# Three token groups' partial sums added by accumulating transfers instead of GpSimd adds, in the selective-scan stage of a graph and state-space block

## The reference, cut to what matters

```
dA = exp(dt[:, :, None] * A[None])                       # 4096 x 512 channels x 16 states
dBu = dt[:, :, None] * B[:, None, :] * u[:, :, None]
def step(hst, inp):
    dAt, dBut, Ct = inp
    hst = dAt * hst + dBut
    return (hst, hst @ Ct)                               # y[token, channel] = sum over 16 states of h * C
y = ys + u * D_skip
y = y * silu(z)
return y @ w_out
```

## Time and profile before

| | |
|---|---|
| median of 3 runs | 2358.94 us |
| the profiled execution, its own time | 2360.41 us |
| its span in the profile | 2358.5 us |
| TensorE busy (matmul) | 2189.1 us, 93% |
| VectorE busy | 1803.0 us, 76% |
| ScalarE busy | 1566.7 us, 66% |
| GpSimd busy | 1146.6 us, 49% |
| scan steps, first to last start | 1106.7 to 2126.4 us |
| mean share of the 16 DMA engines in use, 1186 to 1860 us | about 0.32 |

### The profile page before, as it was taken

How to read it: one execution, slowest core, us unless ns; L and a number is a source line. 1 busy time by engine, 2 the same in 40 slices (tenths; PEclk the granted TensorE clock), 3 DMA queues, 4 the chain that set the end, 5 groups by cost and what they waited for, 6 DMA issues and landing times.

```text
span 2358.5 us, 26231 instructions
## 1 busy us (share of the span) xinstructions
PE 2189.1 (93%) x8900; PEld 1393.1 (59%) x8900; DVE 1803.0 (76%) x2083; ACT 1566.7 (66%) x2541; POOL 1146.6 (49%) x928
## 2 busy tenths in 40 slices
PE   7999999999999999989999999998999987787998
PEld 4544545555555556456766666676766664444886
DVE  5666767777777765324999998999989998996665
ACT  5577686777686845425676767677676868775444
POOL 2101322222231313213988888888988888890000
PEclk9999999999999999999999999999999999898999
DMA  6243332323232323233323232323323221312121
GB/s 234 72 134 102 108 116 90 125 96 122 87 125 88 119 90 134 83 107 109 131 93 125 90 125 89 117 99 107 117 100 125 90 83 43 117 36 98 36 81 45
DMA packets 117495, 241.22 MB, mean 102 GB/s; under 512 B 8770, under 2 KB 66370, under 8 KB 116978
## 3 DMA queue, kind: packets, MB, share of 16 engines
q1 hardware_dynamic: 108290, 207.14, 26.4%
q0 software_dynamic: 8528, 31.36, 3.8%
q10 hardware_dynamic: 544, 1.05, 0.1%
HBM read 219.20 MB, written 20.32 MB: 102 GB/s over the span
## 4 chain that ended last, share of the span: by engine, by line
PE 65%; ACT 10%; POOL 10%; DVE 10%; issue 5%; DMA 0%; ACTq 0%; DVEq 0%; POOLq 0%
PE ps L685 13%; PE ps L727 10%; POOL dB L2306 6%; PE ps L971 5%; DVE h L1473 3%; PE ps L849 2%; PE ps L823 2%; PE ps L955 2%; POOL acc L2288 2%; PE ps L709 2%; ACT ps L1659 2%; ACT L1657 1%; POOL du L2302 1%; PE ps L755 1%; PE ps L753 1%
## 5 line engine op out<-in xcount | busy, mean ns | idle before, releaser
L1473 DVE TENSOR_TENSOR_SCAN h<-ps,hst,dB 128x512 f32<-128x512 f32 x512 | 636.9, 1270 | 59.0 <-ACT ps L1659 50.5
L2306 POOL TENSOR_TENSOR dB<-du,bc 128x512 f32<-128x512 f32 x512 | 648.0, 1287 | 61.6 <-DVE h L1473 59.1
L685 PE MATMUL ps<-wgt,msg 128*128 128x512 f32 x1024 | 489.0, 598 | 2.1 <-DVE xb L1181 2.1
L1659 ACT ACTIVATE ps<-dt,cols 128x512 f32<-128x512 f32 x512 | 351.9, 692 | 181.1 <-DVE h L1473 178.8
L727 PE MATMUL ps<-raw,msg 128*128 128x256 f32 x1792 | 436.3, 379 | 0.9 <-ACT hb L1659 0.9
L971 PE MATMUL ps<-consts,h 128*128 128x128 f32 x2048 | 318.9, 281 | 70.7 <-DVE acc L1435 38.0
L971 PEld LDWEIGHTS ps<-consts,h 128*128 128x128 f32 x2048 | 251.6, 144 | 224.8 <-DVE acc L1435 73.4
L727 PEld LDWEIGHTS ps<-raw,msg 128*128 128x128 f32 x1792 | 324.0, 190 | 74.1 <-issue 42.1
L685 PEld LDWEIGHTS ps<-wgt,msg 128*128 128x128 f32 x1024 | 190.0, 192 | 206.2 <-issue 204.6
L1659 ACT ACTIVATE wgt<-wgt 128x1024 f32<-128x1024 f32 x256 | 257.9, 1046 | 51.9 <-DVE wgt L1146 50.5
L2288 POOL TENSOR_TENSOR acc<-acc,part 128x512 f32<-128x512 f32 x174 | 226.4, 1301 | 59.7 <-ACT part L1659 58.3
(11 more groups left out here) (320 smaller groups left out, 3589.9 us busy)
## 6 DMA issues: line engine op xcount, KB each, us to landing
raw<-in_adjT SPq DMA_DIRECT2D x256, 512.0 KB, 3.4
bc<-tmp_bc SPq DMA_DIRECT2D x64, 512.0 KB, 4.6
E<-tmp_bc POOLq DMA_DIRECT2D x32, 512.0 KB, 4.1
xb<-in_xT POOLq DMA_DIRECT2D x8, 512.0 KB, 4.1
tmp_x<-xb POOLq DMA_DIRECT2D x8, 512.0 KB, 4.2
x<-tmp_x SPq DMA_DIRECT2D x8, 512.0 KB, 5.8
tmp_x<-x SPq DMA_DIRECT2D x8, 512.0 KB, 4.8
msg<-in_W SPq DMA_DIRECT2D x4, 1024.0 KB, 10.6
```

The lines of the kernel that those rows point to most:

```text
L685: x = e.matmul(P[d][:, :], msg[:, j, d * 128:(d + 1) * 128], wgt[g % NW][:, l, :], start=j == 0, stop=j == NJ - 1)
L1473: e.tensor_tensor_scan(hr[n % 3][:, m, :], PS[4 + k % 2].t[:, :], dBr[k % 4][:, :], hst[:, n % 16, m:m + 1], ALU.mult, ALU.add).then_inc(S ...
L1659: return e.activation(out, in_, func, bias=bias, scale=scale)
L2306: e.tensor_tensor(dBr[k % 4][:, :], du[:, m, :], bcr[i % 3][:, n % 2, :], ALU.mult).then_inc(S("dB"), 1)
```

## The change

Parts of groups 0, 1 and 2 are added to `acc` by DMA transfers with an add ("moved"), states 1 to 12 of groups 0 and 1 and states 1 to 11 of group 2. ScalarE writes the parts of all three groups. GpSimd issues the transfers in two chains ("lanes"): groups 0 and 1 in one transfer of two parts, group 2 in one of its own. A transfer is issued at `j + 11` of the last group in its lane; for the last moved state of a lane it is `j + 8`. Each chain has two buffers for parts and one semaphore. To make room, `x3` becomes a view of `xcb` and `th1` becomes `sq1`, with the waits that this needs. `post_b` gets one more slot. Over the whole run 257 units are moved, in 90 transfers of the first lane and 83 of the second; VectorE adds 184, TensorE 40, and ScalarE starts 31.

```diff
@@ adder
-    if s == 0:
-        return "gpsimd" if n < 14 else "vector"
-    if s == 1:
-        return "gpsimd" if 2 <= n < 13 else "vector"
+    if s < 3:
+        return "moved" if n < (13 if s < 2 else 12) else "vector"
     return "vector"
+LANES = ((0, 1), (2,))
+def moved_of(ib, n, lane):
+    return [s for s in LANES[lane] if adder(ib, n, s) == "moved"]
+MOVED = [{x: i for i, x in enumerate((ib, n) for ib in range(NB) for n in range(16) if moved_of(ib, n, lane))} for lane in range(2)]
+def landed(j):
+    ib, n, s = unit(j)
+    return 16 * (MOVED[s // 2][ib, n] + 1)
@@ tiles
-        part = [sb(cB, f"part{i}", [128, 512]) for i in range(2)]
+        part = [[sb(cB, f"part{lane}{i}", [128, len(LANES[lane]), 512]) for i in range(2)] for lane in range(2)]
-        x3 = sb(cB, "x3", [128, 2, TB])
-        th1 = sb(cB, "th1", [128, 2, TB])
+        x3 = xcb[:, 0:2, 3:TB + 3]
+        th1 = sq1
@@ order
-        NP, NPA, NSA, NPB, NPO = 64, 55, 62, 71, 18
+        NP, NPA, NSA, NPB, NPO = 64, 55, 62, 71, 19
-        post_load = [1] * 8 + [0, 0] + mean_var
+        post_load = [1] * 8 + [0, 0] + mean_var + [0]
@@ SyncE, post_b, ahead of the load of x3
+                w.wait_ge(S("halo1"), min(ib + 2, NB))
@@ ScalarE, pre_b, ahead of the write of xcb
                         w.wait_ge(S("halo1"), ib)
+                        w.wait_ge(S("d_xn3"), 16 * (ib - 1))
+                        w.wait_ge(S("sum"), 2 * (ib - 1))
@@ ScalarE, post_b, ahead of the normalization
+                w.wait_ge(S("th1r"), 2 * min(ib + 2, NB))
@@ VectorE, gather
-                        if last in HANDED:
-                            w.wait_ge(S("summed"), HANDED[last] + 1)
+                        if adder(*unit(last)) == "moved":
+                            w.wait_ge(S(f"d_acc{s // 2}"), landed(last))
@@ ScalarE, gather
-                    elif how == "gpsimd":
-                        w.wait_ge(S("summed"), HANDED[j] - 1)
-                        act(part[HANDED[j] % 2][:, :], b.ps[:, :], ACT.Copy, scale=c).then_inc(b.evac, 1)
+                    elif how == "moved":
+                        lane, i = s // 2, MOVED[s // 2][ib, n]
+                        w.wait_ge(S(f"d_acc{lane}"), 16 * (i - 1))
+                        act(part[lane][i % 2][:, s - LANES[lane][0], :], b.ps[:, :], ACT.Copy, scale=c).then_inc(b.evac, 1)
@@ GpSimd
-            def add(j):
-                ib, n, s = unit(j)
-                made, last = hT_use(j), hT_use(j - 4)
-                w.wait_ge(made.evac, made.n)
-                if j - 4 in HANDED:
-                    w.wait_ge(S("summed"), HANDED[j - 4] + 1)
-                else:
-                    w.wait_ge(last.evac, last.n)
-                e.tensor_tensor(acc[:, s, :], acc[:, s, :], part[HANDED[j] % 2][:, :], ALU.add).then_inc(S("summed"), 1)
+            def add(ib, n, lane):
+                ss = moved_of(ib, n, lane)
+                for s in ss:
+                    made, last = hT_use(64 * ib + 4 * n + s), hT_use(64 * ib + 4 * n + s - 4)
+                    w.wait_ge(made.evac, made.n)
+                    if n > 1:
+                        w.wait_ge(S(f"d_acc{lane}"), landed(64 * ib + 4 * n + s - 4))
+                    else:
+                        w.wait_ge(last.evac, last.n)
+                e.dma_start(acc[:, ss[0]:ss[-1] + 1, :], part[lane][MOVED[lane][ib, n] % 2][:, 0:len(ss), :],
+                            accum_op=ALU.add).then_inc(S(f"d_acc{lane}"), 16)
             for k in range(64 * NB + HAND):
-                if k - HAND in HANDED:
-                    add(k - HAND)
+                for behind in (HAND, HAND - 3):
+                    if k >= behind:
+                        ib, n, s = unit(k - behind)
+                        if s < 3 and moved_of(ib, n, s // 2)[-1:] == [s]:
+                            if (behind == HAND) == (n < 15 and (ib, n + 1) in MOVED[s // 2]):
+                                add(ib, n, s // 2)
```

More of the change, by code:

```diff
@@ L48, in unit @@
     return j // 64, j % 64 // 4, j % 4
-HANDED = {j: i for i, j in enumerate(j for j in range(64 * NB) if adder(*unit(j)) == "gpsimd")}
+LANES = ((0, 1), (2,))
[5 more added lines that the diff above has]
+    return 16 * (MOVED[s // 2][ib, n] + 1)
 SUMMED = {j: i for i, j in enumerate(j for j in range(64 * NB) if adder(*unit(j)) == "tensor")}
@@ L440, in build @@
                   (gate_use(NB - 1, 3).full, gate_use(NB - 1, 3).n), (postb_use(NB - 1, 3).evac, postb_use(NB - 1, 3).n),
-                  (S("rr3"), 2 * NB), (S("gate"), 4 * NB), (S("summed"), len(HANDED)), (S("d_x3s"), 16 * NB), (S("d_xn3"), 16 * NB), (S("d_bcs"), 16 * NB)]
+                  (S("rr3"), 2 * NB), (S("gate"), 4 * NB), *((S(f"d_acc{lane}"), 16 * len(MOVED[lane])) for lane in range(2)), (S("d_x3s"), 16 * NB), (S("d_xn3"), 16 * NB), (S("d_bcs"), 16 * NB)]
         @block.sync
@@ L813, in outer @@
                     yield
-                    w.wait_ge(S("setup"), 5)
+                    w.wait_ge(S("setup"), 7)
                     w.wait_ge(Y.evac, Y.n - 1)
@@ L988, in gates @@
                             last, how = hT_use(64 * ib + 60 + s), adder(ib, 15, s)
-                            if how == "gpsimd":
-                                w.wait_ge(S("summed"), HANDED[64 * ib + 60 + s] + 1)
-                            elif how == "tensor":
+                            if how == "tensor":
                                 w.wait_ge(sum_use(ib, s).evac, sum_use(ib, s).n)
@@ L1117, in _ @@
             w.wait_ge(S("d_consts"), 32)
-            e.tensor_copy(col("cw0", 16, 4)[64:128, :], col("cw0", 20, 4)[0:64, :]).then_inc(S("taps"), 1)
-            e.tensor_copy(col("cb0", 4)[64:128, :], col("cb0", 5)[0:64, :]).then_inc(S("taps"), 1)
+            e.tensor_copy(col("cw0", 16, 4)[64:128, :], col("cw0", 20, 4)[0:64, :]).then_inc(S("setup"), 1)
+            e.tensor_copy(col("cb0", 4)[64:128, :], col("cb0", 5)[0:64, :]).then_inc(S("setup"), 1)
             w.wait_ge(S("Aexp"), 1)
@@ L1210, in pre_a @@
                 e.scalar_tensor_tensor(dt, sm[:, 2, :], 0.0, sm[:, 3, :], ALU.max, ALU.add).then_inc(S("dt"), 1)
-                w.wait_ge(S("setup"), 1)
+                w.wait_ge(S("setup"), 3)
                 w.wait_ge(S("dt"), ib + 1)
@@ L1220, in pre_a @@
                     w.wait_ge(b.evac, b.n)
-                    w.wait_ge(S("taps"), 2)
+                    w.wait_ge(S("setup"), 2)
                     e.tensor_scalar(c, xbc[:, m, 0:TB], col("cw0", 4 * m), col("cb0", m), ALU.mult, ALU.add).then_inc(S("conv"), 1)
```

## The result

The changed kernel takes **2431.76 us** (median of 4 runs, 2429.82 to 2433.62) against 2359.43 for the kernel before beside it: a ratio of **1.0306** (95% interval 1.0288 to 1.0324). It is slower, as forecast, but by 72 us where 12 were forecast, and above the upper end of its range, 2396.

What follows compares the result with a forecast made beforehand. TensorE was taken to bound the long stretches, GpSimd and VectorE full at 1337 to 1374 us. Six blocks at +2.4 us (+14.4), block 6 -1.9, block 7 -4.3 and +4.2: +12.4, so 2371 us; range from a little under 2334 to 2396.

Steps and rivals of the forecast that it cites:

- last transfer of the first lane: Step 49, iteration 57: GpSimd has time by then, counted at 0, up to 2 us; landings counted hidden.
- Last transfer of group 2: Step 46, issued in iteration 54: `dB` of step 54 waits for ScalarE's part and the issue, +2.6 us a block.
- ScalarE's parts: 11 more per block at 0.7 us, hidden in TensorE's stretches; the one at step 49 costs +0.3 us.
- -0.7 for the short chain: One add fewer on VectorE shortens the ScalarE and VectorE chain before 1416.0 us, -0.7 us a block.
- `post_b`'s +0.5: Two sums move from the block's end to step 25, beside the short chain: 0 to 1.2 us, taken as +0.5.
- An issue: On GpSimd, taken as 0.57 us like a plain one, other end 1.31; GpSimd 18 us lighter a block.
- rival D: GpSimd is not relieved: an issue costs 1.3 us, as an add did; 2376 us, no chance given.
- VectorE's adds: Per block 36 become 25, 8 us less, mostly worth nothing under TensorE or ScalarE; -0.7 and +0.7 us counted.
- Blocks 6 and 7: Block 6, not TensorE-bound: -1.9 us. Block 7: six adds off full VectorE -4.3, two late last transfers +4.2.
- Shared tiles: New waits for `x3` in `xcb` and `th1` in `sq1` are for work already finished in program order: 0.
- A: Rival, faster: late `dB` of step 54 is covered by ScalarE's bound, the full stretch shrinks; 2334 us, chance 0.35.
- C: Rival: transfers land after more than 8.3 us behind two adjacency loads; 2413 us at 9 us, chance 0.07.

Runs made afterwards that it cites:

- e5: Against e1, group 2's adds go back to VectorE, leaving only the first lane's transfers, last ones at 11: 2371.55 us, ratio 1.0058.
- e1: Against the changed kernel, the last transfer of each lane is issued 11 steps behind its unit instead of 8: 2378.39 us, ratio 1.0087.
- e7: Against the changed kernel, only the first lane's last transfer goes to 11 steps behind, group 2's stays at 8: 2412.21 us, ratio 1.0224.
- e11: Against e5, the first lane's last transfer is issued 8 steps behind its unit, group 2 still on VectorE: 2380.27 us, ratio 1.0089.
- e4: Against the kernel before, only the shared tiles, their waits and the extra post slot, no accumulating transfer: 2360.67 us, ratio 1.0009.
- e8: Against the kernel before, group 2 moved by transfers at 11 in blocks 6 and 7 only, GpSimd's adds kept: 2359.32 us, ratio 1.0002.

## Why the prediction was wrong

**The step that failed** is the last transfer of the first lane, by way of its landing: "A chain's next transfer waits for the one before, four steps later (8.3 us at 133.1 / 64) ... I count it hidden", and "The first lane's last one (step 49, iteration 57) ... I count it at 0, up to 2 us". The distance of four steps holds for all transfers of a lane but the last, and the last is issued three iterations early, as the paragraph before it in the prediction says. 11 - 8 = 3 of the four steps are gone. One step is 2.1 us; by that sum even the 4.2 us of a plain transfer would have left 2.1 where 0 was counted. What came in its place is a landing of 8.66 us, most of it in the open, and an idle VectorE of 6.7 us, of which 2.8 a block remain in the time.

This is the largest of three terms that were too small. Taken one step at a time, the runs split the block like this (us a block):

| part of the change | in the prediction | measured |
|---|---|---|
| first lane at 11, shared tiles (e5 less before) | -0.7 - 0.3 + 0.7 + 0.5 = +0.2 | 133.5 - 133.1 = +0.4 |
| group 2's lane, at 11 (e1 less e5) | +0.3 - 0.7 = -0.4 | 135.8 - 133.5 = +2.3 |
| group 2's last transfer at 8 (e7 less e1) | +2.6 | 139.9 - 135.8 = +4.1 |
| first lane's last transfer at 8 (changed kernel less e7) | 0 | 142.7 - 139.9 = +2.8 |
| sum | +2.4 | +9.6 |

Point by point:

- **First lane's last transfer, 0.** Wrong: 2.8 a block on top of group 2's, 1.7 alone (e11). Two things were left out. One is the landing, 5.1 us of the wait at step 57. The other is the row of exponential, part, issue and `dB` that the prediction had found at step 54: at step 57 it makes the scan 3.3 us late by itself in e11, where the landing ends together with the part, and the softplus addition did not cover it.
- **Last transfer of group 2, +2.6.** The mechanism was right, at the step named, and the size too small: the scan is 3.3 us late, where 2.5 were counted (3.3 was the end with the dear issue), and the early issue costs 4.1 a block. The sum left out that the issue also slows the `dB` behind it (1.88 us in the row at 1351.35, 1.29 counted). Why 3.3 us late costs 4.1 is not shown.
- **ScalarE's parts, +0.3, "in TensorE's stretches they are hidden".** Too small. With the -0.7 for the short chain, group 2's lane was counted at -0.4 a block and measured at +2.3; the scans' wait for the exponential grows with it (37.1 to 52.6 us in 850). `post_b`'s +0.5 is in line with e4's block of 133.6, though that execution was 3.7 us slower than e4's median.
- **An issue, 0.57, with 1.31 as the other end.** The next instruction starts 0.61 us after the issue (1347.69 to 1348.30), but the next `dB` takes 0.3 to 0.6 longer: 0.9 to 1.2 us of GpSimd in all, nearer rival D's end. `dB`'s mean rose from 1291 ns to 1503. GpSimd's busy time in a block fell to 528.8 / 5 = 105.8, not to 98: it is 10 us lighter, not 18.
- **VectorE's adds.** 184 are left, as said, and its idle time grew by more than what they took. That this relief is worth little in blocks 0 to 5 is in line with the runs (group 2's lane, which brings it, costs 2.3 us a block), but none isolates it.
- **Blocks 6 and 7, -1.9 and six adds for -4.3.** Block 6 became 9.0 us longer, and block 7 with what follows 7.0. e8 measures the move of group 2 in these two blocks, with its parts and issues, at nothing. That TensorE is not full in block 6 (107 of 133 us) was read as if VectorE's adds then counted, and VectorE's 110 of 115 in block 7 as if each add did; neither shows in e8.
- **Shared tiles, 0.** Right alone (e4); with the transfers VectorE waits 2.5 us a block for the store, and e5 shows no price for the like (10.0 us in six blocks, the block within 0.4 us of before).
- **The two long stretches stay TensorE-bound.** Right where it was read: from 1300 to 1337 us TensorE is busy 36.83 of 37.00.

**The rivals.** A (faster) needed the late `dB` to be covered; nothing covered it. C had the landing as its cause and 2413 as its time, so it was nearest, and the prediction's own sign for it (a block near 140, landings in the chain) was seen. But the road is another: C wanted landings over 8.3 us all along the chain, and 158 of 173 took no more than that. They hurt where the distance is one step. That the mechanism of C also has a point in the list where it needs no slow landing is what a table of issue iterations (unit 45 at 56, unit 49 at 57) would have shown. D's price of an issue was nearly right, but its time was 2376.

**Left open.** Why the landing of state 11's transfer takes 8.66 us here and 6.6 in e11 is not settled; e11 was to tell whether group 2's transfer just ahead of it is the cause (then near 5.4, else near 8), and 6.6 lies between. In the changed kernel the landing falls together with two loads of 512 KB, as the DMA view from 1350 to 1357 us shows. But e11's had three such loads beside it, and no run took them away:

```profile
DMA packets 829, 1.54 MB, mean 221 GB/s; under 512 B 49, under 2 KB 561, under 8 KB 829
...
acc<-part POOLq DMA_DIRECT2D x1, 512.0 KB, 8.7
```

## What to carry to other kernels

When work goes from an engine to transfers that the same engine issues in order, the landing becomes a wait in that engine's instruction stream: write down for each chain the iteration of every issue, its last and first ones above all, and hold the smallest distance against the slowest landing, not the usual distance against the median. Do the same with what the issue itself waits for: an early issue that meets its data just in time makes all behind it late, even when the landing adds almost nothing (e11). Shortening the distance of the last one to save latency downstream undoes this exactly there. And busy time taken off an engine need not be time gained: here it was 51 us on GpSimd and 39 on VectorE in five blocks, and even with both last transfers at 11 the block is 2.7 us longer than before.

## What was not expected of the hardware

- **An addition with two SBUF inputs on VectorE, beside GpSimd.** The same softplus addition (128x1024) takes 1.22 us in one place and 3.37 or 4.97 (e7) in others. In e1, VectorE:

```profile
1344.84 3.37 DVE L1393 TENSOR_TENSOR dt<-dt,sq 128x1024 f32<-128x1024 f32 x1
...
1356.67 1.22 DVE L1393 TENSOR_TENSOR dt<-dt,sq 128x1024 f32<-128x1024 f32 x1
```

and GpSimd:

```profile
1342.90 4.22 POOL L2323 TENSOR_TENSOR dB<-du,bc 128x512 f32<-128x512 f32 x3
...
1354.33 1.27 POOL L2323 TENSOR_TENSOR dB<-du,bc 128x512 f32<-128x512 f32 x1 [0.56 <-DVE h L1482]
1357.97 1.26 POOL L2319 TENSOR_TENSOR du<-dt,u 128x512 f32<-128x512 f32 x1 [2.37 <-DVE dt L1393]
```

  It is long beside `dB` in a row and short where GpSimd waits. That is only seen together; no run took `dB` away. The Trainium skill (SBUF, State Buffer, section "Who interferes with whom") says that such an instruction contends with a GpSimd one that reads SBUF; the rows agree, and give a size of 2 to 3.8 us where the prediction had counted 0.3.

- **Landings with an add.** 512 KB took 5.4 us and 256 KB 4.2 in the median, and 4.4 and 3.2 at the least: 1.2 us for 256 KB more, no more than the 1.4 us of plain ones. The spread is large: the slowest took 10.3 us.

- **TensorE's clock after a stall.** Windows of the changed kernel, columns as above:

```profile
1345.00:1363.00 18.00, 9.37 (x49) 6.81 (x47) 7.00 (x7) 11.30 (x22) 8.62 (x9) 0.87 0.70 178
1363.00:1373.00 10.00, 8.82 (x41) 7.54 (x42) 9.89 (x12) 5.35 (x11) 8.51 (x8) 0.71 0.25 69
1373.00:1400.00 27.00, 24.61 (x136) 19.41 (x134) 27.00 (x31) 16.49 (x26) 21.11 (x18) 1.00 0.36 118
```

  After 18 us in which TensorE was busy for 9.4, the granted clock is 0.71 in the next 10 us: part of them at 1.2 GHz, not 2.4. Cut finer, TensorE stands idle from 1357 to 1363 us; the granted clock is 1.00 up to 1357, 0.75 from there to 1360, 0.50 to 1366, 0.54 to 1369 and 1.00 again after that. In the kernel before, the first two of these windows stand at 1.00 and the third at 0.94. Over the five blocks TensorE took 12 us more for the same 3066 instructions (636.19 against 624.19). VectorE is full in those 10 us (9.89), so little of it should lie on the path; no run tested that.
